# Alignment of 32 sequences: from rows on 32 partitions to four column blocks on 128

## The chip, the cores and the metric

One Trainium2 chip, one core of it. The metric is the device time of one execution in microseconds (us). Engines: PE is TensorE, DVE VectorE, ACT ScalarE, POOL GpSimd, SP SyncE, whose queue issues most DMAs.

## The reference

Two layers with four residual branches over x (32 sequences x 128 tokens x 128) and a context of the same shape:

```python
x = x + tanh(g_xattn[0]) * mlstm(layernorm(x), ctx, ctx)            # 8 heads of 16
x = x + tanh(g_ffn[0])   * quantized_ffn(layernorm(x))              # 128 -> 512 -> 128
x = x + tanh(g_xattn[1]) * align(ctx, layernorm(x))                 # the part that changes
x = x + tanh(g_ffn[1])   * experts(layernorm(x))                    # 8 experts, 128 -> 512 -> 128
```

`align`, for each of the 32 sequences: D[i,j] is the Euclidean distance between context token i and token j of the layer-normed x. R is the dynamic time warping cost, R[i,j] = D[i,j] + min(R[i-1,j], R[i,j-1], R[i-1,j-1]). A backtrack from (127,127) takes the best of diagonal, up and left (in this order when equal), and each row i of the context is added to every column j that the path visits in row i.

## The kernel before, in words

All of x stays in SBUF (`xs`), tokens on partitions. Engines run hand-written programs, each in its own written order, and wait on semaphores. The stages follow one another: mLSTM, quantized ffn, alignment, experts (the second half of the time). The alignment goes like this:

- **Squared distances** (PE L1420 to L1445, ACT L629 to L640, DVE L1052 to L1056). For each group g of four sequences PE turns the layer-normed x, ACT makes -2x and x squared of it (L636, L637), PE sums them with the context, DVE adds the context's norms into `dsq`. ACT takes the root (L640) into `dist`, with tokens i on the partitions. In ACT's order the root of group g-1 stands before the copies of group g+1.
- **Turning** by DRAM: SP writes `dist` to `d_scratch` (L338) and reads it back with the sequences on 32 partitions (`distances`, L334) into `dring`.
- **Row loop** (DVE L1064 to L1088). 128 rows; each is a minimum of the row above with itself shifted by one (L1077) and a `tensor_tensor_scan` with (min, add) over 128 columns (L1081), both on 32 partitions. Each waits for the other's semaphore.
- **Step table** (`back`, L262 to L293). Rows are taken in chunks of 32, 32, 32, 16, 16. SP copies finished rows to 128 partitions, a quarter of the chunk on each 32 (`r9`, L353, L355). DVE then makes MIN, DIAG, LEFT (comparisons), GpSimd the code `ch_k` (L485, L486), DVE a scan with (max, max) (SCAN, L284) and a difference (CUT, L292), which SP brings back to 32 partitions as `kb` (L260). `back_part` puts these parts, of 128 columns each, one behind each minimum and one behind each scan of the next chunk's rows. The last chunk's table is made behind the loop (L1089 to L1100).
- **Tracking** (DVE L1102 to L1110): 128 dependent steps, each a `scalar_tensor_tensor` over 128 columns of `kb` whose sum is the column at which the next row's path ends.
- **Path and sum** (L1111 on): PE turns the ends (L1455), ACT and DVE make 0/1 paths, PE multiplies them with the context (L1463), DVE adds, and the layer norm of the last branch begins.

Beside it the expert weights are prepared (16 tiles of 128x512): ACT issues the loads (`raw_load`, L247), PE turns them (L1452) into banks 4 and 5, ACT copies them to SBUF (L647), GpSimd splits each into a high and a low bf16 part (L475, L476). This begins when the squared distances are done and runs beside the first rows of the loop. Later, `low` (L495) is GpSimd's part of the experts.

Of the kernel before, what the change touches and what calls it, by code (L numbers as in the profile page):

```python
# [5 lines left out]
F32 = mybir.dt.float32  # L6
BF16 = mybir.dt.bfloat16
# [12 lines left out]
E = 8  # L20
# [8 lines left out]
RC = 32  # L29

CHUNKS = [(0, 32), (32, 32), (64, 32), (96, 16), (112, 16)]
NRC = len(CHUNKS)
R9 = 5 * 16


MIN, DIAG, LEFT, SCAN, CUT = range(5)
PLACE_0 = 7
BACK = [sum(5 * rows // 4 for _, rows in CHUNKS[:c]) for c in range(NRC)]
LEFT_DONE = [BACK[c] + 3 * CHUNKS[c][1] // 4 for c in range(NRC - 1)] + [BACK[-1] + 3]
CUT_DONE = [BACK[c] + 5 * CHUNKS[c][1] // 4 for c in range(NRC - 1)] + [BACK[-1] + 6 + CHUNKS[-1][1] // 4]  # L40
# [4 lines left out]
RW = P + 1  # L45


def program(nc, x, ctx_, g_x, g_f, if_w, if_b, on_w, a_w1, a_b1, a_w2, a_b2, gate_w, m_w1, m_b1, m_w2, m_b2, out):
    with ExitStack() as stack:
# [5 lines left out]

        def dram(name, shape, dt):
            return nc.dram_tensor(name, shape, dt)
# [36 lines left out]
        xT2 = Bm[:, 0:1024].rearrange("p (s t) -> p s t", s=2)  # L94
        xTsq = Bm[:, 1024:2048].rearrange("p (s t) -> p s t", s=2)
        dsq = Bm[:, 2048:6144].rearrange("p (b j) -> p b j", b=B)
        dist = Bm[:, 6144:10240].rearrange("p (b j) -> p b j", b=B)

        dring = A[:, 0:8192].rearrange("p (s r j) -> p s r j", s=2, r=RC)
        kb = A[:, 8192:16384].bitcast(BF16).rearrange("p (i j) -> p i j", i=P)  # L100
        rring = Bm[:, 0:2 * (RC + 1) * RW].rearrange("p (s r j) -> p s r j", s=2, r=RC + 1)
        o0 = 2 * (RC + 1) * RW
        r9 = Bm[:, o0:o0 + 9 * RW].rearrange("p (r j) -> p r j", r=9)
        o0 += 9 * RW
        ch_m = Bm[:, o0:o0 + 1024].rearrange("p (r j) -> p r j", r=8)
        ch_g = Bm[:, o0 + 1024:o0 + 2048].rearrange("p (r j) -> p r j", r=8)
        ch_k = Bm[:, o0 + 2048:o0 + 3072].rearrange("p (r j) -> p r j", r=8)
        ch_s = Bm[:, o0 + 3072:o0 + 3072 + 8 * RW].rearrange("p (r j) -> p r j", r=8)
        o0 += 3072 + 8 * RW
        ch_d = Bm[:, o0:o0 + 512].bitcast(BF16).rearrange("p (r j) -> p r j", r=8)  # L110
# [19 lines left out]
        iota2 = sb("iota2", [P, P])  # L130
        ones = sb("ones", [P, P])
# [53 lines left out]
        wraw = slab[:, 0:1024].rearrange("p (s c) -> p s c", s=2)  # L185
        wcp = slab[:, 1024:2048].rearrange("p (s c) -> p s c", s=2)
# [9 lines left out]

        d_dram = dram("d_scratch", (B, P, P), F32).ap()
# [13 lines left out]
            "x3T_turned", "x3T_kept", "dsum_done", "dsq_ready", "dist_ready", "row_done", "rowm_done",  # L211
            "r9_in", "back_done", "k_made", "k_in",
            "track_done", "e_turned", "e_kept", "far_ready", "path_ready", "expanded", "expanded_added",
            "raw_turned", "raw_kept", "w_split",
# [5 lines left out]
        d_out = [sem(f"d_out{c}") for c in range(2)]  # L220
        d_in = [sem(f"d_in{c}") for c in range(2)]
        k_last = [sem(f"k_last{q}") for q in range(4)]
        raw_in = [sem(f"raw_in{c}") for c in range(2)]
# [23 lines left out]
        def raw_load(act, n):  # L247
            if n < E:
                dst, src = four(wraw[:, n % 2, :]), m_w1[n].rearrange("(c p) d -> p c d", c=NC)
            else:  # L250
                dst, src = wraw[:, n % 2, :], m_w2[n - E]
            act.dma_start(dst, src).then_inc(raw_in[n % 2], 16)

        def steps_out(sp, c, parts=range(3, -1, -1)):
            first, rows = CHUNKS[c]
            h = rows // 4
            sp.wait_ge(S["back_done"], CUT_DONE[c])
            for q in parts:
                arrived = S["k_in"] if c < NRC - 1 else k_last[q]
                sp.dma_start(kb[0:B, first + h * q:first + h * q + h], ch_d[32 * q:32 * q + 32, 0:h]).then_inc(arrived, 16)  # L260

        def back(dve, c, stage, q0, q1):  # L262
            h = CHUNKS[c][1] // 4
            q = slice(q0, q1)
            end = c == NRC - 1

            def after(stage):
                dve.wait_ge(S["back_done"], BACK[c] + (stage if end else stage * h + q0) + 1)
            if stage == MIN:
                if q0 == 0:  # L270
                    dve.wait_ge(S["r9_in"], R9 * (c + 1))
                    if c >= 1:
                        dve.wait_ge(S["k_made"], c)
                ins = dve.tensor_tensor(ch_m[:, q], r9[:, q0:q1, 0:P], r9[:, q0:q1, 1:RW], ALU.min)
            elif stage == DIAG:
                ins = dve.tensor_tensor(ch_g[:, q], r9[:, q0:q1, 0:P], r9[:, q0:q1, 1:RW], ALU.is_le)
            elif stage == LEFT:
                after(MIN)
                ins = dve.tensor_tensor(ch_m[:, q], r9[:, q0 + 1:q1 + 1, 0:P], ch_m[:, q], ALU.is_ge)
            elif stage == SCAN:  # L280
                if not end:
                    dve.wait_ge(S["k_made"], c + 1)
                ks = ch_k[:, q].rearrange("p r j -> p (r j)")
                ins = dve.tensor_tensor_scan(ch_s[:, q, 1:RW].rearrange("p r j -> p (r j)"), ks, ks, 0.0, ALU.max, ALU.max)  # L284
            else:
# [4 lines left out]
                if c >= 1:  # L290
                    dve.wait_ge(S["k_in"], 64 * c)
# [1286 lines left out]
```

## Time and profile before

| | us |
|---|---|
| median of 3 runs | 946.1 |
| lowest, highest | 945.65, 1039.48 |
| the profiled execution | 947.22 |
| its span, first to last instruction | 945.5 |
| mean granted TensorE clock in it | 0.804 |

All rows are of the profiled execution; their times count from the start of the span. "32x128 f32" is partitions x elements. A busy time of a group is the union over its instructions; idle time in brackets names the instruction that ended it. PE, PEld (weight load), DVE, ACT and POOL are engines, SPq and ACTq are the queues of SP and ACT that issue DMAs. An fp32 product appears as two records.

### The profile page before, as it was taken

The page shows a single profiled execution, that of the slowest core. Times are in us where ns is not written, and L with a number is a line of the kernel's source. Part 1 is how long each engine was busy: PE and PEld are TensorE (multiplying, and loading weights), DVE is VectorE, ACT ScalarE, POOL GpSimd, SP SyncE. Part 2 cuts the span into 40 slices and gives each one's busy share as a digit, 9 for nine tenths or more (in the row PEclk, how much of TensorE's full clock was granted, in tenths as well). Part 3 has the DMA queues.
Part 4 walks back from the last instruction along what each step waited for, and adds up shares of the span by engine and source line. Part 5 has one row for each costly group of instructions (what it writes and reads, how often), then busy time and mean ns, then how long its engine had stood idle before and what let it go on. Part 6 is the DMA issues. An engine that isn't in the chain of part 4 may idle for free.

```text
span 945.5 us, 16592 instructions
## 1 busy us (share of the span) xinstructions
PE 630.7 (67%) x5620; PEld 432.7 (46%) x5701; DVE 719.7 (76%) x2023; ACT 384.6 (41%) x688; POOL 246.8 (26%) x253
## 2 busy tenths in 40 slices
PE   5968999942525832000000068999999999999998
PEld 4943444421214521000000058677756777777776
DVE  6655678787989569999979885656665878878675
ACT  2344555538852421000000043656554454545453
POOL 1001687851435065201210004877400000000000
PEclk9998999975555955555555565999999999999999
DMA  7000000000000262111110000000000000001000
GB/s 187 23 1 1 1 0 0 0 0 0 1 23 1 79 161 68 41 46 37 25 25 0 0 1 1 1 3 1 2 1 1 13 13 1 11 0 34 0 12 13
DMA packets 26122, 19.61 MB, mean 21 GB/s; under 512 B 2004, under 2 KB 23760, under 8 KB 25936
## 3 DMA queue, kind: packets, MB, share of 16 engines
q1 hardware_dynamic: 20592, 14.65, 6.0%
q10 hardware_dynamic: 5472, 4.26, 1.8%
q8 instruction: 28, 0.46, 0.2%
q14 instruction: 30, 0.25, 0.1%
HBM read 11.21 MB, written 4.19 MB: 16 GB/s over the span
## 4 chain that ended last, share of the span: by engine, by line
PE 57%; DVE 35%; ACT 3%; issue 3%; DMA 2%; SPq 0%; POOL 0%; ACTq 0%; DVEq 0%; POOLq 0%
PE PS L1488 7%; DVE Bm L1081 7%; PE PS L1503 6%; PE PS L1505 6%; PE PS L1504 6%; PE PS L1489 6%; DVE rowm L1077 5%; DVE rowm L1108 5%; PE PS L1487 4%; PE PS L1370 4%; PE PS L1288 3%; PE PS L1344 2%; DVE A L708 2%; DVE hmm L1006 2%; DVE hmm L1007 2%
## 5 line engine op out<-in xcount | busy, mean ns | idle before, releaser
L671 ACT ACTIVATE A<-PS,small_t 128x512 f32<-128x512 f32 x256 | 168.6, 688 | 123.0 <-PE PS L1489 121.5
L1503 PE MATMUL PS<-kT_w,A 128*128 128x128 bf16 x1024 | 174.8, 219 | 0.0
L1504 PE MATMUL PS<-kT_w,A 128*128 128x128 bf16 x1024 | 174.7, 219 | 0.0
L1505 PE MATMUL PS<-kT_w,A 128*128 128x128 bf16 x1024 | 174.7, 219 | 0.0
L1202 DVE TENSOR_TENSOR A<-A 128x512 bf16<-128x512 f32 x192 | 123.6, 690 | 10.5 <-ACT A L671 9.2
L1455 PE MATMUL PS<-identf,ee 32*128 32x32 f32 x1 | 0.3, 312 | 176.6 <-DVE rowm L1108 176.6
L1503 PEld LDWEIGHTS PS<-kT_w,A 128*128 128x128 bf16 x1024 | 100.2, 98 | 11.3 <-issue 4.5
L1504 PEld LDWEIGHTS PS<-kT_w,A 128*128 128x128 bf16 x1024 | 100.2, 98 | 6.6
L1488 PE MATMUL PS<-A,xn_w 128*128 128x512 bf16 (+1 forms) x256 | 97.8, 382 | 3.6 <-issue 0.4
L1505 PEld LDWEIGHTS PS<-kT_w,A 128*128 128x128 bf16 x1024 | 100.2, 98 | 0.0
L1489 PE MATMUL PS<-A,xn_w 128*128 128x512 bf16 (+1 forms) x256 | 97.8, 382 | 0.0
L1210 DVE SCALAR_TENSOR_TENSOR xs<-PS,A,xs 128x128 f32 (+1 forms) x192 | 54.0, 344 | 55.8 <-PE PS L1505 55.8
L653 ACT ACTIVATE Bm<-iota,ec 128x128 f32<-128x128 f32 x32 | 9.5, 386 | 177.4 <-DVE ec L708 177.4
L1455 PEld LDWEIGHTS PS<-identf,ee 32*128 32x128 f32 x1 | 0.2, 178 | 177.0 <-DVE rowm L1108 177.0
L1487 PE MATMUL PS<-A,xn_w 128*128 128x512 bf16 (+1 forms) x193 | 73.8, 382 | 0.0
L495 POOL TENSOR_TENSOR A<-A 128x512 bf16<-128x512 f32 x64 | 64.5, 1041 | 23.3 <-ACT A L671 23.3
L1081 DVE TENSOR_TENSOR_SCAN Bm<-rowm,A 32x128 f32<-32x128 f32 x128 | 67.2, 525 | 2.6
L870 DVE TENSOR_TENSOR Bm<-Bm,PS 128x512 f32<-128x512 f32 x64 | 43.9, 686 | 33.0 <-PE PS L1344 29.6
L1077 DVE TENSOR_TENSOR rowm<-Bm 32x128 f32<-32x128 f32 x128 | 48.6, 380 | 6.9 <-DMA A<-d_scratch 4.4
L572 ACT ACTIVATE Bm<-PS 128x512 f32<-128x512 f32 x64 | 38.2, 597 | 26.2 <-PE PS L1362 26.2
L1108 DVE SCALAR_TENSOR_TENSOR rowm<-iota,ee,A 32x128 f32<-32x128 f32 x128 | 43.5, 340 | 6.3 <-DMA A<-Bm 1.8
L1370 PE MATMUL PS<-slab 32*128 32x256 f32 x256 | 45.9, 435 | 0.0
(273 smaller groups left out, 1332.4 us busy)
## 6 DMA issues: line engine op xcount, KB each, us to landing
slab<-in_L_ffn_w_dram ACTq DMA_DIRECT2D x16, 256.0 KB, 3.0
xs<-in_x_dram SPq DMA_DIRECT2D x4, 512.0 KB, 6.0
cs<-in_ctx_dram SPq DMA_DIRECT2D x4, 512.0 KB, 6.7
d_scratch<-Bm SPq DMA_DIRECT2D x8, 256.0 KB, 2.3
out_dram<-xs SPq DMA_DIRECT2D x8, 256.0 KB, 2.5
Bm<-Bm SPq DMA_DIRECT2D x9, 145.1 KB, 2.4
A<-d_scratch SPq DMA_DIRECT2D x2, 512.0 KB
A<-d_scratch SPq DMA_DIRECT2D x2, 384.0 KB
```

The source lines that it names most:

```text
L671: act.activation(hf[:, e % 2, c, :], bank(c), ACT.Gelu_apprx_tanh, bias=b1).then_inc(S["h_gelu"], 1)
L1077: dve.tensor_tensor(rowm[:], above[:, 1:RW], above[:, 0:P], ALU.min).then_inc(S["rowm_done"], 1)
L1081: dve.tensor_tensor_scan(rring[0:B, c % 2, r + 1, 1:RW], rowm[:], dring[0:B, i // RC % 2, i % RC], BIG, ALU.min, ALU.add)\
L1108: dve.scalar_tensor_tensor(out=rowm[:], in0=iota2[0:B], scalar=ee[:, i + 1:i + 2], in1=kb[0:B, i, :], op0=ALU.is_le, op1=ALU.mult, accum_o ...
L1202: dve.tensor_tensor(hl[:, e % 2, c, :], hf[:, e % 2, c, :], hh[:, e % 2, c, :], ALU.subtract).then_inc(S["h_low_dve"], 1)
L1370: ins = pe.matmul(PS[:, 2 + 2 * half + jj, 0:256], kslot[r, k % 2, :], qslot[r, k % 2], start=True, stop=True)
L1487: pe.matmul(bank(c), w1h[:, e, c, :], x4h[:, xw], start=True, stop=False)
L1488: pe.matmul(bank(c), w1h[:, e, c, :], x4l[:, xw], start=False, stop=False)
L1489: pe.matmul(bank(c), w1l[:, e, c, :], x4h[:, xw], start=False, stop=True).then_inc(S["h_ready"], 1)
L1503: pe.matmul(o, hh[:, e % 2, c, t], w2h[:, e, c, :], start=(c == 0 and k == 0), stop=False, skip_group_check=True)
L1504: pe.matmul(o, hh[:, e % 2, c, t], w2l[:, e, c, :], start=False, stop=False, skip_group_check=True)
L1505: ins = pe.matmul(o, hl[:, e % 2, c, t], w2h[:, e, c, :], start=False, stop=(c == NC - 1), skip_group_check=True)
```

## The change

- **Blocks.** The 128 columns are cut into four blocks of 32, block q on partitions 32q to 32q+31. Block q runs 4q steps behind block 0 (`LAG` = 4), so the loop has 128 + 12 = 140 steps of 128 partitions x 32 columns. The scan's start value is the column 0 of the new row in the table `rt`, in which the last column of the block to the left stands. ACT brings it there: three copies of 32 partitions x 2 rows every two steps (`pass_edges`), for which DVE waits at every second step from step 4 on.
- **Distances.** `dsq` stays as it is and PE turns it: 128 fp32 products with a shifted identity (`idw`), stationary `dsq[:, :, 32q+j]` (a stride of 128 elements), 140 moving columns, four products for the four groups of 32 output partitions, three j to a PSUM bank, 11 banks' worth in four banks. ACT takes the root out of PSUM into `dd`, 11 instructions. The DRAM scratch and its DMAs are gone, and the root no longer stands in the loop over g.
- **Step table.** Made in place, on the same 128 partitions, out of `rt` and the kept minima (`mins`): no MIN part and no `r9`. Chunks of 32, 32, 32, 18, 12, 10, 4 steps. A part is now one instruction for the whole chunk. The code is made by GpSimd for the first four chunks and by DVE for the last three; so is the difference (`steps_of`), before on DVE. A scan with (mult by `resets`, max) gives each block its own maximum; ACT passes the last columns on to the blocks to the right (`pass_tops`, six copies), and DVE joins them (CARRY, TOP). SP brings the differences to `kb`, now in four blocks (q, i, j).
- **Tracking** reads `kb[0:B, :, i]`, four blocks of 32. It waits once, for all of the table.
- **Weights.** SP issues the loads, four buffers. PE turns with products that stay open, ACT copies the high part as bf16, PE subtracts it in PSUM (with a negative identity, `identn`), ACT copies the rest. All but the first two turns come after the row loop in ACT's order. GpSimd has no part in it.
- GpSimd sets up `idw`, `cq`, `rt`, `g_t` and `resets` with memsets during the quantized ffn.

```diff
+LAG = 4
+EACH = 2
+NSTEP = P + 3 * LAG
+CHUNKS = [(0, 32), (32, 64), (64, 96), (96, 114), (114, 126), (126, 136), (136, 140)]
+ON_POOL = 4
+SCAN_AT = [12, 12, 12, 8, 4, 3, 0]
+TOP_AT = [16, 16, 16, 11, 7, 0, 0]
...
+            if stage == DIAG:
+                dve.wait_ge(S["row_done"], b)
+                ins = dve.tensor_tensor(g_t[:, 0:n, 1:RTW], diag, up, ALU.is_le)
             elif stage == LEFT:
+                ins = dve.tensor_tensor(l_t[:, 0:n], left, mins[:, a:b], ALU.is_ge)
...
+                ins = dve.tensor_tensor_scan(flat(top_t[:, 0:n]), flat(resets[:, 0:n]), flat(g_t[:, 0:n]), 0.0, ALU.mult, ALU.max)
+            elif stage == CARRY:
...
+                ins = dve.tensor_reduce(top_t[:, 0:n, 0], cq[:, :, a:b].rearrange("p n s -> p s n"), AX, ALU.max)
+            elif stage == TOP:
+                dve.wait_ge(done, back_at(c, CARRY))
+                ins = dve.tensor_tensor(top, top, carry.to_broadcast([P, n, QC]), ALU.max)
...
+        def back_part(dve, s):
+            for c, (a, b) in enumerate(CHUNKS[:-1]):
+                r = s - b
+                if r == TOP_AT[c] and c < NRC - 2:
+                    back(dve, c, CARRY)
+                    back(dve, c, TOP)
+                    if c >= ON_POOL:
+                        back(dve, c, CUT)
+                for n, stage in enumerate((DIAG, LEFT, CODE, KEEP)):
+                    if r == n and (n < 2 or c >= ON_POOL):
+                        back(dve, c, stage)
+                if r == SCAN_AT[c]:
+                    back(dve, c, SCAN)
...
+            for c in range(ON_POOL):
+                pool.wait_ge(S["back_done"], back_at(c, LEFT))
+                link(code(pool, c))
+                keep_code(pool, c).then_inc(S["k_made"], 1)
+                pool.wait_ge(S["back_done"], back_at(c, TOP))
+                steps_of(pool, c)
...
+            for n in range(TURNS):
+                j0, j1 = JB * n, min(JB * n + JB, QC)
+                act.wait_ge(S["d_turned"], n + 1)
+                own = bank(4 + n % 4, 0, NSTEP * (j1 - j0)).rearrange("p (j s) -> p j s", s=NSTEP)
+                act.activation(dd[:, :, j0:j1].rearrange("p s j -> p j s"), own, ACT.Sqrt).then_inc(S["dist_kept"], 1)
...
+                for q in range(3):
+                    ins = act.activation(rt[32 * q + 32:32 * q + 64, s0 + LAG + 1:s1 + LAG + 1, 0], rt[32 * q:32 * q + 32, s0 + 1:s1 + 1, QC], ACT.Copy)
+                ins.then_inc(S["edge_kept"], 1)
...
+            for s in range(NSTEP):
+                if s:
+                    dve.wait_ge(S["row_done"], s)
+                dve.tensor_tensor(mins[:, s], rt[:, s, 1:RTW], rt[:, s, 0:QC], ALU.min).then_inc(S["min_done"], 1)
+                back_part(dve, s)
+                if s >= LAG and (s - LAG) % EACH == 0:
+                    dve.wait_ge(S["edge_kept"], (s - LAG) // EACH + 1)
+                dve.wait_ge(S["min_done"], s + 1)
+                dve.tensor_tensor_scan(rt[:, s + 1, 1:RTW], mins[:, s], dd[:, s], rt[:, s + 1, 0:1], ALU.min, ALU.add).then_inc(S["row_done"], 1)
...
+            pe.wait_ge(S["turn_ready"], 1)
+            pe.wait_ge(S["dsq_ready"], G4)
+            for n in range(TURNS):
+                if n >= 4:
+                    pe.wait_ge(S["dist_kept"], n - 3)
+                for j in range(JB * n, min(JB * n + JB, QC)):
+                    for q in range(4):
+                        o = NSTEP * (j - JB * n)
+                        ins = pe.matmul(PS[32 * q:32 * q + 32, 4 + n % 4, o:o + NSTEP], dsq[:, :, QC * q + j],
+                                        idw[:, (3 - q) * LAG:(3 - q) * LAG + NSTEP], start=True, stop=True)
+                ins.then_inc(S["d_turned"], 1)
```

## Rows read from the trace of the kernel before

**Rows 1.** Windows: us, busy of PE, PEld, DVE, ACT, POOL, PEclk, DMA share, GB/s

```profile
339.50:369.00 29.50, 11.48 (x44) 8.12 (x44) 28.08 (x41) 7.17 (x12) 21.88 (x25) 0.50 0.45 111
...
339.50:484.10 144.60, 11.48 (x44) 8.12 (x44) 139.30 (x396) 7.17 (x12) 38.67 (x33) 0.50 0.21 50
...
493.60:542.90 49.30, 0.26 (x2) 0.26 (x2) 44.50 (x256) 0.00 (x0) 0.00 (x0) 0.50 0.01 1
```

**Rows 2.** Timeline of DVE, a bare row: start us, length us, line, shapes

```profile
377.35 0.28 DVE L1077 TENSOR_TENSOR rowm<-Bm 32x128 f32<-32x128 f32 x1
377.67 0.41 DVE L1081 TENSOR_TENSOR_SCAN Bm<-rowm,A 32x128 f32<-32x128 f32 x1
378.11 0.28 DVE L1077 TENSOR_TENSOR rowm<-Bm 32x128 f32<-32x128 f32 x1
```

**Rows 3.** Timeline of DVE, a row with two table parts

```profile
389.53 0.27 DVE L1077 TENSOR_TENSOR rowm<-Bm 32x128 f32<-32x128 f32 x1
389.73 0.27 DVE L279 TENSOR_TENSOR Bm<-Bm 128x128 f32<-128x128 f32 x1
389.93 0.41 DVE L1081 TENSOR_TENSOR_SCAN Bm<-rowm,A 32x128 f32<-32x128 f32 x1
...
390.45 0.27 DVE L1077 TENSOR_TENSOR rowm<-Bm 32x128 f32<-32x128 f32 x1
```

**Rows 4.** Timeline, a chunk's code on GpSimd beside the loop

```profile
391.93 2.39 POOL L485 TENSOR_TENSOR Bm<-iota,Bm 128x1024 f32<-128x1024 f32 x1 [23.20 <-DVE Bm L279]
392.21 2.25 DVE L1077 TENSOR_TENSOR rowm<-Bm 32x128 f32<-32x128 f32 x1
...
394.50 2.52 DVE L1081 TENSOR_TENSOR_SCAN Bm<-rowm,A 32x128 f32<-32x128 f32 x1
```

**Rows 5.** Groups of DVE, by form: count, busy us, mean ns, idle before

```profile
L870 DVE TENSOR_TENSOR Bm<-Bm,PS 128x512 f32<-128x512 f32 x64 | 43.9, 686 | 33.0 <-PE PS L1344 29.6 <-ACT Bm L572 3.3
...
L279 DVE TENSOR_TENSOR Bm<-Bm 128x128 f32<-128x128 f32 x28 | 7.0, 266 | 0.0
...
L718 DVE TENSOR_TENSOR lnt<-lnt 128x16 f32<-128x16 f32 x8 | 1.4, 169 | 0.0
...
L708 DVE TENSOR_SCALAR hpos<-hidf,pm 128x8 f32<-128x8 f32 x1 | 0.2, 231 | 0.0
...
L708 DVE TENSOR_SCALAR hneg<-hpos 128x8 f32<-128x8 f32 x1 | 0.2, 171 | 0.0
```

**Rows 6.** Groups of POOL, by form

```profile
L495 POOL TENSOR_TENSOR A<-A 128x512 bf16<-128x512 f32 x64 | 64.5, 1041 | 23.3 <-ACT A L671 23.3
```

**Rows 7.** Groups of ACT, by form

```profile
L515 ACT ACTIVATE lnt<-lnt,cst 128x16 f32<-128x16 f32 x8 | 2.5, 306 | 24.4 <-DVE lnt L720 24.3
...
L522 ACT ACTIVATE tg<-tgr 128x4 f32<-128x4 f32 x1 | 0.2, 205 | 7.4 <-DVE tgr L791 7.4
```

**Rows 8.** Timeline of the squared distances; brackets: idle before, and what ended it

```profile
310.72 1.05 PE L1437 MATMUL PS<-Bm,kT_w 128*128 128x128 f32 x8
...
312.70 0.63 ACT L640 ACTIVATE Bm<-Bm 128x512 f32<-128x512 f32 x1 [5.16 <-DVE Bm L708]
...
314.36 1.12 PE L1434 MATMUL PS<-Bm,ones 128*128 128x512 f32 x2 [2.15 <-ACT Bm L637]
...
328.34 1.13 DVE L708 TENSOR_SCALAR Bm<-PS,aa 128x128 f32<-128x128 f32 x4 [1.06 <-PE PS L1437]
```

**Rows 9.** Timeline of PE in the mLSTM: four products of 32 output rows

```profile
171.89 0.43 PE L1344 MATMUL PS<-Bm 128*32 128x128 f32 x8
172.25 0.33 PE L1351 MATMUL PS<-identf,Bm 128*128 128x128 f32 x1
```

**Rows 10.** The page, granted clock in 40 slices of 23.6 us, in tenths

```profile
PEclk9998999975555955555555565999999999999999
```

**Rows 11.** Timeline behind the last row

```profile
486.25 0.69 DVE L274 TENSOR_TENSOR Bm<-Bm 128x512 f32<-128x512 f32 x1 [2.15 <-DMA Bm<-Bm]
...
491.76 1.42 ACTq L260 DMA_DIRECT2D A<-Bm  x2
```

More of the change, by code:

```diff
@@ L293, in back @@
[L293 to L308 removed]
+                else:
+                    dve.wait_ge(done, back_at(c, KEEP))
@@ new lines, in _, with high, rest @@
+            act.wait_ge(S["rt_ready"], 1)
+            for e in range(GROUPS):
+                pass_edges(e)
+                for c, (a, b) in enumerate(CHUNKS[:-1]):
+                    if e == min((b + SCAN_AT[c] - EACH) // EACH, GROUPS - 1):
+                        pass_tops(c)
+            def high(n):
+                act.wait_ge(S["raw_turned"], n + 1)
+                act.activation(weights(n)[0][:, n % E], four(bank(4 + n % 4)), ACT.Copy).then_inc(S["raw_kept"], 1)
+            def rest(n):
+                act.wait_ge(S["w_left"], n + 1)
+                act.activation(weights(n)[1][:, n % E], four(bank(4 + n % 4)), ACT.Copy).then_inc(S["w_split"], 1)
@@ L650, in _ @@
+            for n in range(2 * E + 1):
+                if n < 2 * E:
+                    high(n)
+                if n >= 1:
+                    rest(n - 1)
             act.wait_ge(S["e_kept"], 1)
@@ L1098, in _ @@
-            for q in range(h):
-                back(dve, c, SCAN, q, q + 1)
-            back(dve, c, CUT, 0, h)
-            for i in reversed(range(P)):
-                first, rows = CHUNKS[-1]
-                if i >= first and (P - 1 - i) % (rows // 4) == 0:
-                    dve.wait_ge(k_last[(i - first) // (rows // 4)], 16)
-                elif i == first - 1:
-                    dve.wait_ge(S["k_in"], 64 * (NRC - 1))
-                dve.scalar_tensor_tensor(out=rowm[:], in0=iota2[0:B], scalar=ee[:, i + 1:i + 2], in1=kb[0:B, i, :],
+            dve.memset(ee[:], 2.0 * (P - 1))
@@ new lines, in _ @@
+            for stage in (DIAG, LEFT):
+                back(dve, NRC - 1, stage)
+            for stage in (CARRY, TOP, CUT):
+                back(dve, NRC - 2, stage)
+            for stage in (CODE, KEEP, SCAN, CARRY, TOP, CUT):
+                back(dve, NRC - 1, stage)
+            for c in (NRC - 2, NRC - 1):
+                dve.wait_ge(k_in[c % 2], K_IN[c])
+            cols = lambda t: t.rearrange("p (q j) -> p q j", q=4)
+            for i in reversed(range(P)):
+                dve.scalar_tensor_tensor(out=cols(rowm[:]), in0=cols(iota2[0:B]), scalar=ee[:, i + 1:i + 2], in1=kb[0:B, :, i],
```

342 lines of the change are left out of this document (144 added, 198 removed).

## The prediction

> **What bounds the kernel now.** I read the stages first, in a table of windows chosen where the work changes [rows 1]. The alignment is one stretch on DVE: 144.6 us for the row loop (DVE busy 139.3 of them, PE 11.5, ACT 7.2), then about 9.5 us that finish the step table, then 49.3 us of tracking with DVE busy 44.5 and every other engine idle. So in this stretch DVE's order is the path, and nothing that PE or ACT do there has a price unless DVE waits for it. The timeline then says what the 144.6 us are made of. A bare row is a minimum of 0.28 us and a scan of 0.41 us, each waiting for the other: 0.76 us from minimum to minimum [rows 2], 97.3 us for 128 rows. Table parts of 128x128 between them cost less than they last: minimum to table part 0.20, to scan 0.20, scan with a second part 0.52, so 0.92 us for a row with two of them, 0.08 each [rows 3]. And twice in a chunk DVE stands still: a minimum that starts during a GpSimd instruction of 2.39 us lasts 2.25 instead of 0.28, the scan behind it 2.52 instead of 0.41 [rows 4]. That is 4.1 us a chunk, three times, and 1.9 for the half chunk: 14 us. The same happens in the first 29.5 us, where GpSimd is busy 21.9 us splitting weights [rows 1]: 20 rows are made there that bare would take 15.2, so another 14 us. Some 28 us of the loop are GpSimd in DVE's way; rows 97, table parts the rest.
>
> **The row loop.** 128 rows of 32x128 become 140 steps of 128x32. A minimum: from 128 to 512 elements a two-input instruction goes from 0.266 to 0.686 us [rows 3, 5], 1.09 ns an element, so 96 elements fewer give 0.278 - 0.105 = 0.173; a 16-wide one measures 0.169 [rows 5], which says that it can't go much lower. I take 0.178. The scan is the term with two readings. At 128 wide it lasts 0.133 more than the minimum [rows 2], which is 1.04 ns an element, the price of one more element-time each; it would be a coincidence if it were a fixed part. So I take 0.411 - 2 x 0.100 = 0.211; with a fixed part it would be 0.311. New is that its start value is read from a column of the table instead of a constant; a scalar from memory shows in two 8-wide instructions, 0.231 with and 0.171 without [rows 5]: plus 0.060. Gaps of 0.032 and 0.035 stay [rows 2]. Step: 0.178 + 0.032 + 0.271 + 0.035 = 0.516 us, x 140 = 72.2 us. Bounds: 0.456 without the 0.060 (64 us) and 0.616 with the fixed part (86 us).
> The Trainium skill ("DVE: opcode table, instruction layouts, handler registers and perf-mode slots", Datapath and trigger behaviour) says that the scan runs at half throughput; this trace has one width and can't show it, but by it the reading per element holds. It also has a rule against this change: "VectorE: DVE Perf Modes", The TRN2 errata, says that many small tiles pay a fixed 151 cycles each; by (32 + 151)/0.96 a minimum would be 191 ns, and the loop 1.8 us longer than here, an estimate; at 128 the same formula gives 291 where the trace has 266 to 278.
>
> **Table parts on DVE.** They now take a whole chunk in one instruction: 32 steps are 1024 elements. In front of a scan there are 0.210 us (minimum to scan, dependent) of which an independent 32-wide one needs about 0.10 [rows 2, 3], so a part of N elements adds about N x 1.04 ns - 0.04: DIAG 1.02, LEFT 1.02, SCAN of 1056 at two element-times 2.16, CARRY with TOP behind it 1.28, together 5.5 us for a chunk of 32. Three such chunks 16.5; the chunk of 18 steps 3.1; that of 12, which makes its code on DVE too, 3.2; that of 10 as far as it lies in the loop 1.8. Sum 24.6 us. Nothing of the old MIN part remains, since the loop keeps its minima.
>
> **GpSimd beside it.** The weight split leaves GpSimd (it becomes PE products and ACT copies after the loop), so the first 14 us of standstill go. But the step code of four chunks stays there and gets a third instruction, the difference (steps_of). Each reads SBUF while DVE runs two-input instructions, which is the case of [rows 4]. Per full chunk 1.97 + 2.11 + 1.97 = 6.05 us, three times 18.2, and 3.1 for the chunk of 18: 21.3 us. Bounds: zero if the new bf16 operands changed the stalling, though the operand count, not the type, is what the stalled rows share; and if the bf16 instructions cost like the one of 512 elements at 1.041 us [rows 6] against 1.2 for half of the 2.39 one, 18 us. I keep 21.3.
>
> **Hand-overs through ACT.** Every second step DVE waits for three ACT copies of 32x2 that carry the edge to the next block. Queued behind this waiting scan is all of DVE's loop. From the row's end to the scan that needs it lie two steps and a minimum, 1.24 us (2 x 0.516 + 0.21). The smallest ACT instruction here is 0.205, a 16-wide one with a root 0.306 [rows 7]; three with two hand-offs of 0.08 are 0.8 to 1.1. Hidden, price 0; without cover it is 68 times the excess. The six copies that carry the table's maxima stand before the next edges in ACT's queue, 1.2 to 1.8 us against four steps (2.1): I give 1 us in all. Loop: 72.2 + 24.6 + 21.3 + 1.0 = 119.1 us against 144.6, **-25.5**.
>
> **Ahead of the loop.** Before, squared distances went through a root on ACT, out to DRAM and back; the last DVE piece of them ends at 329.5 [rows 8] and the loop began at 339.5. Two things move. First, the root stood in ACT's order ahead of the next group's copies: ACT idled 5.16 us for DVE, and PE's product waited 2.15 for ACT [rows 8]. With the roots gone this wait goes, late next is PE itself: squared distances end at 327.3. Shorter waits of later groups I leave out. Second, the turning: 128 fp32 products of 32 output rows, in 32 sets of four with one set of array columns each. The nearest row is the same shape, 128x32 against 128x128: four of them (eight records) take 0.43 us, and the next instruction on the whole array starts 0.36 after the first [rows 9]. For 140 columns 0.39: 32 x 0.39 = 12.5 us. The clock was full (9 tenths) up to that point and PE doesn't pause before it [rows 10]. ACT's 11 roots of 420 elements run beside it at half PE's time; the last adds 0.8 with hand-offs. DVE starts at 327.3 + 12.5 + 0.8 = 340.6, plus 0.3 for the constants added at the start: **+1.4**. Bounds: -2 if sets overlap more; +24 if they run one after another, below.
>
> **The end of the table.** From the last scan (484.1) to the first tracking step it was 9.5 us: 2.15 of waiting for a DMA, table work to 491.7, 1.8 for the DMA home [rows 1, 11]. Now eleven short DVE instructions of 128 to 320 elements, 3.6 us by the prices above; then the last of five DMAs from SP. Four of them are issued 1.9 us before the last table part is ready, at 0.71 us each [rows 11], so the fifth goes 0.9 later and lands 1.9 after that: 6.4 us. **-3.0**.
>
> **Tracking and weights.** The tracking instruction reads four blocks of 32 instead of one of 128. A two-block product elsewhere has the price of a flat one (0.686 for 512) [rows 5], so 0. Bound: +0.1 us a step, 13 us. The 16 weight tiles now pass PE (four fp32 products, 1.05 us at full clock [rows 8], 2.1 at half, and one bf16 product) and two ACT copies of 0.6: 16 x 2.5 = 40 us at half clock, beside 49.3 us of tracking in which both idle [rows 1]. Hidden; had they been exposed they would cost what exceeds 49.
>
> **Sum.** +1.4 - 25.5 - 3.0 = -27.1 us. The profiled execution took 947.22 (span 945.5); it becomes 920.1. The median of the runs is 946.1, 1.1 lower: **919.0 us**. A measurement of this kernel can tell about 2% from no change, that is below 927 or above 965.
>
> **Rivals.**
> (a) The scan's extra is a fixed part, or short instructions cost 0.1 more: +14 for the steps, -4.7 for table scans that get cheaper: 928. For it: no narrow scan in the trace. Against: the coincidence above.
> (b) GpSimd doesn't stop DVE any more: 919 - 21 = 898. For it: operands in bf16. Against: both stalled instructions of [rows 4], and the stalls in the weight split, whose outputs were bf16 already.
> (c) The turning runs set by set without overlap: four full-array fp32 products of 128 columns take 1.05 us at full clock [rows 8], with 140 columns 1.15, so 32 x 1.15 = 36.8 instead of 12.5: 943. For it: the strided stationary operand, which no row has.
> (d) Tracking pays for four blocks: +13, 932.
> (e) The slower side: ACT's edge copies pace the loop. Two steps need 1.03 us; from 0.29 us a copy (3 x 0.29 + 0.16) ACT's own order is longer and each of 68 pairs takes its time. At 0.52 a copy a pair takes 1.72: 68 x 0.69 = 47 us, 966. For it: nothing in the trace moves data between partition groups on ACT. Against: 0.205 and 0.306 [rows 7].
>
> **Chances.** Forecast 0.55 (its own range 908 to 928); (a) 0.13, (b) 0.12, (d) 0.08, (c) 0.06, (e) 0.06. Leaving out most of (b)'s far side, (c) and (e), the range is 900 to 941. Faster: most of the forecast, all of (b), a third of (a), 0.68; within 2%: 0.26; slower: (e), 0.06.
>
> **What would show it.** Right: 128x32 scans near 0.27 and minima near 0.18 with 0.52 between steps; minima or scans of about 2.2 us exactly when GpSimd runs, three times a chunk; PE's turning 12 to 13 us long; no DVE wait for ACT. Wrong: DVE idle before scans with ACT as releaser (e), steps of 0.6 and more (a), 128-partition scans undisturbed beside GpSimd (b), turning sets of 1 us (c), tracking over 0.39 us a step (d), or a PE wait after tracking for the weights.

## The result, and the profile after

The changed kernel takes 917.1 us (three runs, 915.39, 917.12 and 918.83) against 945.65 and 946.1 before: a ratio of 0.9696 [0.9652, 0.9739], 3.0% faster, with 919.0 forecast and 900 to 941 as the range. A second comparison gave 916.25 to 917.31 and 0.9686 [0.9658, 0.9714]. Both kernels also have executions some 93 us longer (1037.88 and 1039.48 before, 1009.62 and 1010.02 after, again 29 us apart), which the forecast left out and which no ratio here uses.

The profiled execution of the changed kernel (1010.02 us, span 1008.2) held the half clock through the mLSTM, well ahead of the alignment, so its alignment begins 92.1 us later than before, while lengths inside it compare directly. The page shows it in the granted clock, where [rows 10] had nines:

```profile
PEclk9995555555555555955555856599999999999999
```

The stages of the alignment as windows (us, busy of PE, PEld, DVE, ACT, POOL, PEclk, DMA share, GB/s): from the last squared distance to the first minimum, the loop of 140 steps, the end of the table, and tracking.

```profile
418.57:428.11 9.54, 7.92 (x257) 7.70 (x257) 0.13 (x2) 8.27 (x11) 0.00 (x0) 1.00 0.02 5
428.11:549.65 121.54, 2.00 (x16) 1.81 (x16) 108.86 (x314) 49.15 (x236) 20.95 (x12) 0.52 0.03 9
549.65:556.00 6.35, 4.23 (x18) 3.94 (x19) 3.12 (x11) 3.91 (x11) 0.00 (x0) 0.50 0.05 12
556.00:606.00 50.00, 16.21 (x110) 14.57 (x111) 44.72 (x257) 14.55 (x27) 0.00 (x0) 0.67 0.22 64
```

Against [rows 1]: the loop is 121.4 us instead of 144.6 (the window closes 0.1 late) and still DVE's; ACT, nearly idle before, is now busy for 49 us of it. Tracking has 44.7 us of DVE against 44.5, with the weights on PE and ACT beside it.

A step without table parts, timeline of DVE (start, length, line, shapes), to be held against [rows 2]:

```profile
454.18 0.19 DVE L1104 TENSOR_TENSOR A<-Bm 128x32 f32<-128x32 f32 x1
454.47 0.28 DVE L1109 TENSOR_TENSOR_SCAN Bm<-A,Bm 128x32 f32<-128x32 f32 x1
454.79 0.19 DVE L1104 TENSOR_TENSOR A<-Bm 128x32 f32<-128x32 f32 x1
455.02 0.28 DVE L1109 TENSOR_TENSOR_SCAN Bm<-A,Bm 128x32 f32<-128x32 f32 x1
455.34 0.19 DVE L1104 TENSOR_TENSOR A<-Bm 128x32 f32<-128x32 f32 x1
```

A step is 0.55 us. Every second one is 0.61: the first scan here starts 0.29 behind its minimum, the other 0.23. The first is the one that waits for the edge as well, and the edge has long been there. No view lists this as a wait, but the trace has an instruction of DVE's queue for it, on the line of the wait for the minimum, 68 times and only ahead of scans that wait for two semaphores (the line's view: shortest, median, longest ns, first and last start):

```profile
L1108 DVEq EVENT_SEMAPHORE  x68: 21/21/21, 430.5 to 547.6; - x68
```

It shows as 0.067 us at 52 of the 68 places. At the other 16 a table part stands between minimum and scan and hides it.

GpSimd beside the loop, timeline of both engines (brackets: idle before, and what ended it), as in [rows 4]:

```profile
449.52 1.96 POOL L266 TENSOR_TENSOR Bm<-iotaq,Bm 128x1024 bf16<-128x1024 bf16 x1 [56.26 <-DVE A L289]
...
449.66 1.86 DVE L1104 TENSOR_TENSOR A<-Bm 128x32 f32<-128x32 f32 x1
451.55 1.96 POOL L270 TENSOR_TENSOR Bm<-Bm,A 128x1024 bf16<-128x1024 bf16 x1
451.63 1.97 DVE L1109 TENSOR_TENSOR_SCAN Bm<-A,Bm 128x32 f32<-128x32 f32 x1
...
464.88 1.89 POOL L276 TENSOR_TENSOR Bm<-A 128x1024 bf16<-128x1024 f32 x1 [11.37 <-DVE A L311]
465.03 1.79 DVE L1104 TENSOR_TENSOR A<-Bm 128x32 f32<-128x32 f32 x1
```

Three GpSimd instructions a chunk, and each holds a DVE instruction of 0.19 or 0.28 until it ends. What it costs stands in the groups of DVE in the loop (count, busy us, mean ns, idle before):

```profile
L1109 DVE TENSOR_TENSOR_SCAN Bm<-A,Bm 128x32 f32<-128x32 f32 x140 | 45.4, 324 | 7.6
L1104 DVE TENSOR_TENSOR A<-Bm 128x32 f32<-128x32 f32 x140 | 38.4, 274 | 14.2 <-ACT A L647 9.4
L303 DVE TENSOR_TENSOR_SCAN A<-Bm 128x1056 f32<-128x1056 bf16 x3 | 7.1, 2350 | 0.0
L311 DVE TENSOR_TENSOR A<-A 128x1024 f32<-128x1024 f32 x3 | 3.7, 1226 | 0.1
L287 DVE TENSOR_TENSOR Bm<-Bm 128x1024 bf16<-128x1024 f32 x3 | 3.7, 1218 | 0.0
```

Undisturbed, 140 scans of 0.284 and 140 minima of 0.192 are 66.6 us; they last 83.8, so 17.2 us are standstill.

The way into the loop: DVE's last squared distances, ACT's roots, DVE's first minimum (timeline), and PE's turning (the line's view: shortest, median, longest ns, first and last start).

```profile
417.45 1.12 DVE L746 TENSOR_SCALAR Bm<-PS,aa 128x128 f32<-128x128 f32 x4 [0.63 <-PE PS L1450]
...
419.74 8.27 ACT L647 ACTIVATE A<-PS 128x420 f32<-128x420 f32 x11 [4.71 <-PE PS L1468]
...
428.11 0.19 DVE L1104 TENSOR_TENSOR A<-Bm 128x32 f32<-128x32 f32 x1 [9.41 <-ACT A L647]
```

```profile
L1468 PE MATMUL PS<-A,Bm x256: 282/283/348, 418.7 to 426.3; 128*32 128x140 f32 x128
```

The 32 sets take 7.9 us, 0.246 each, so three sets, one root's worth, take 0.72. ACT's 11 roots run without a gap and start every 0.77, a little slower than that, and they end 1.4 us behind PE's last product. One root is longer than the distance between two of them, since they overlap (the line's view; the short one is the last, of 280 elements):

```profile
L647 ACT ACTIVATE A<-PS x11: 663/975/1012, 419.7 to 427.3; 128x420 f32<-128x420 f32 x10, 128x280 f32<-128x280 f32 x1
```

ACT's groups around the loop, and behind it the end of the table (timeline; SPq is SP's queue):

```profile
L653 ACT ACTIVATE Bm<-Bm 32x2 f32<-32x2 f32 x204 | 41.6, 204 | 62.2 <-DVE Bm L1109 60.4
```

```profile
545.54 9.50 SPq L362 DMA_DIRECT2D A<-Bm  x7
...
549.25 0.26 DVE L1109 TENSOR_TENSOR_SCAN Bm<-A,Bm 128x32 f32<-128x32 f32 x1
...
550.73 0.19 DVE L308 TENSOR_REDUCE A<-A 128x10 f32<-128x30 bf16 x1 [0.69 <-ACT A L664]
...
556.25 0.34 DVE L1121 SCALAR_TENSOR_TENSOR rowm<-iota,ee,A 32x128 f32<-32x128 f32 x1 [2.55 <-DMA A<-Bm]
```

An edge copy is 0.204 us. From the last scan (549.5) to the first tracking step it is 6.7 us instead of 9.5, the last 2.55 of them for the DMA that brings the table home.

The three stages together: ahead of the loop, from PE's second turn of four sequences (305.33 before, 397.44 here) to the first minimum, 34.2 us became 30.7 (-3.5); the loop -23.2; the end of the table -2.8. Sum -29.5; the runs say -29.0. Nothing is left for the rest: tracking lasts 49.03 us in both traces, and from its end to the end of the program it is 402.9 in both.

### The profile page after: what moved, and what is told of

Its sections match the earlier page's. It is cut to its first block, busy times and chain, and to the rows that moved or that the text cites. A ratio compares the mean times of both kernels' runs of the same rounds, so it can differ in the third digit from the quotient of the medians.

```text
span 1008.2 us, 17409 instructions
## 1 busy us (share of the span) xinstructions
PE 738.0 (73%) x5953; PEld 475.6 (47%) x6037; DVE 677.2 (67%) x1940; ACT 447.1 (44%) x947; POOL 225.2 (22%) x234
## 4 chain that ended last, share of the span: by engine, by line
PE 59%; DVE 25%; issue 4%; ACT 3%; SPq 0%; DMA 0%; DVEq 0%; POOL 0%; ACTq 0%; POOLq 0%
PE PS L1383 7%; PE PS L1526 7%; PE PS L1541 6%; PE PS L1542 6%; PE PS L1543 6%; PE PS L1527 5%; DVE Bm L1109 5%; DVE rowm L1121 5%; PE PS L1525 4%; DVE A L1104 4%; PE PS L1357 4%; PE PS L1373 3%; PE PS L1375 3%; PE PS L1364 2%; PE PS L1372 2%
## 5 line engine op out<-in xcount | busy, mean ns | idle before, releaser
L1478 PE MATMUL PS<-identf,slab 128*128 128x128 f32 x128 | 20.2, 311 | 125.3 <-ACT xn_w L676 121.7
L1383 PE MATMUL PS<-slab 32*128 32x256 f32 x256 | 78.3, 710 | 0.2 <-DVE slab L746 0.2
L653 ACT ACTIVATE Bm<-Bm 32x2 f32<-32x2 f32 x204 | 41.6, 204 | 62.2 <-DVE Bm L1109 60.4
L1484 PEld LDWEIGHTS PS<-xn_w,identn 128*128 128x128 bf16 x8 | 1.0, 125 | 121.4 <-ACT xn_w L676 121.4
L1383 PEld LDWEIGHTS PS<-slab 32*128 32x128 f32 x256 | 32.3, 308 | 53.4 <-DVE Bm L910 29.3
L567 ACT ACTIVATE Bm<-PS 128x128 f32<-128x128 f32 x64 | 17.8, 278 | 74.2 <-PE PS L1357 74.2
L1109 DVE TENSOR_TENSOR_SCAN Bm<-A,Bm 128x32 f32<-128x32 f32 x140 | 45.4, 324 | 7.6
```

The lines of the kernel that those rows point to most:

```text
L1109: dve.tensor_tensor_scan(rt[:, s + 1, 1:RTW], mins[:, s], dd[:, s], rt[:, s + 1, 0:1], ALU.min, ALU.add).then_inc(S["row_done"], 1)
L1383: ins = pe.matmul(PS[:, 2 + 2 * half + jj, 0:256], kslot[r, k % 2, :], qslot[r, k % 2], start=True, stop=True)
```

## The experiments

Each ran beside the kernel before on the same chip.

**The change again**, for a narrower interval and beside the first variants.

> The changed kernel itself, for a second profile. Theory: about 917 us; PE's turning 7.9 us and 9.5 us from the last squared distance to the first minimum, the loop 121.5 us, 6.6 us from the last scan to tracking, as in its first profile, since nothing in these stretches depends on PE's clock before them. Rival: the first profile's mLSTM ran at the half clock (the record says 5 tenths there), and if that state lasts into the alignment, then these stretches get shorter here, by up to half of PE's 7.9 us.

917.31, 916.72 and 916.25 us, as said above. The other runs are held against 917. The second trace has the lengths of the first: 7.9 us of turning, 9.5 from the last squared distance to the first minimum, 121.4 for the loop, 6.7 for the end of the table. Its mLSTM ran at the half clock too, so by itself it can't answer the rival; the trace of the version with all parts together, further down, has the full clock in most of its mLSTM and the same 7.9 us of turning.

**GpSimd out of the loop.** The step code of all chunks on DVE.

```diff
-ON_POOL = 4
+ON_POOL = 0
```

> ON_POOL = 0: DVE makes the code and the differences of all chunks, GpSimd nothing in the loop. Theory (a GpSimd instruction that reads SBUF stops DVE's two-input instructions for its whole length): the standstills of 1.77 + 1.77 + 1.60 us a full chunk go (1.86 and 1.97 and 1.79 instead of 0.19, 0.28, 0.19), 15.4 us for three and about 2.6 for the chunk of 18, 18 in all; DVE takes on three instructions a chunk, the two bf16 ones at 0.33 us for 320 elements, so about 0.6 us of issue for 1024, and the f32 difference 1.1: 2.3 a full chunk, 8.2 in all. Net -9 to -11 us, about 907. Rival (the standstill only replaces waiting that DVE would do anyway, for ACT's edges or its own results): the work added counts in full and the time rises by about 8, to 925.

907.03 us, and 905.85 on the repeat below. Groups of DVE:

```profile
L1109 DVE TENSOR_TENSOR_SCAN Bm<-A,Bm 128x32 f32<-128x32 f32 x140 | 39.4, 281 | 7.0
L1104 DVE TENSOR_TENSOR A<-Bm 128x32 f32<-128x32 f32 x140 | 26.9, 192 | 14.1 <-ACT A L647 9.3
...
L276 DVE TENSOR_TENSOR Bm<-A 128x1024 bf16<-128x1024 f32 x3 | 3.7, 1225 | 0.1
L266 DVE TENSOR_TENSOR Bm<-iotaq,Bm 128x1024 bf16<-128x1024 bf16 x3 | 2.1, 701 | 0.0
```

The pairs lose 17.5 us (83.8 to 66.3). What comes back on DVE: twelve instructions, 2.63 us for each full chunk and 1.68 for the fourth, 9.6 in all; each starts under the instruction before it and fills a gap, which is worth some 0.2 (at the end of the loop a part of 0.48 adds 0.28 between minimum and scan). So 7.2 come back by this reckoning, 10.3 are gained, and the runs show 10 to 11; the loop itself is 111.7 us in both traces of this version against 121.4, 9.7 less. The standstill is shown, and so is that it costs more than the work it was meant to save.

**The weights alone.** The kernel before, with nothing changed but the weight split, taken to PE and ACT as in the change (four buffers, as there) and left beside the loop. The code shows a part of the edit; PE's products are not in it.

```diff
+            pool.tensor_scalar(identn[:], identb[:], -1.0, 0.0, ALU.mult, ALU.add)
...
-            for n in range(2 * E):
-                split_weights(n)
...
-                act.activation(wcp[:, n % 2, :], bank(4 + n % 2), ACT.Copy).then_inc(S["raw_kept"], 1)
+                act.activation(weights(n)[0][:, n % E], four(bank(4 + n % 4)), ACT.Copy).then_inc(S["raw_kept"], 1)
...
+            def rest(n):
+                act.wait_ge(S["w_left"], n + 1)
+                act.activation(weights(n)[1][:, n % E], four(bank(4 + n % 4)), ACT.Copy).then_inc(S["w_split"], 1)
```

> The kernel before with one part of the change alone: the expert weights are split by PE and ACT (four buffers, loads still issued by ACT, done beside the row loop) instead of by GpSimd. Theory: the 20 rows that took 29.5 us take 15.2, so -14 us: 932, which is half of the whole gain. Rival (the new alignment alone brings the gain; the weights beside it only used time in which DVE waited for its own results): within 3 us of 946.

932.55, 934.84 and 935.84 us, ratio 0.9873 [0.9828, 0.9918], 12 us less. The window of its row loop, to be held against the 144.60 of [rows 1]:

```profile
339.10:469.40 130.30, 15.15 (x82) 12.95 (x82) 125.04 (x396) 10.16 (x19) 16.78 (x8) 0.54 0.20 48
```

The loop is 14.3 us shorter with its rows unchanged. Ahead of it this version is 2.4 us slower than before (41.9 us from PE's first turn to the first minimum, against 39.4), which leaves the 12 of the runs; why it is slower there stays open. Of the change's 29 us, then, 12 to 14 are not owed to the four blocks at all, but to GpSimd's leaving the first 29.5 us of the loop. The blocks, the turning and the table in place bring the other 15 to 17.

**Edges every four steps.** Half as many hand-overs, but the copies then have no step between them and the scan that needs them.

```diff
-EACH = 2
+EACH = 4
```

> EACH = 4: the edge is handed on every fourth step, with the same lag of four, so the hand-over has a minimum as its only cover. Theory: three copies at 0.21 us spacing and two hand-offs are 0.8 us from the end of the scan to the next permitted one; 0.23 of it lie beside the minimum, so about 0.55 us are exposed at 34 places, +19, less 34 second waits of 0.06, -2: +14 to +18 us, about 933. Rival (the copies, not their latency, are what ACT's path is short of; half as many instructions are quicker): within 3 us of the changed kernel or faster.

926.02 and 926.06 us, ratio 0.9784: 9 more than the change, half of what was expected. Waits of DVE, and one of them in the timeline:

```profile
DVE Bm L1109 <- ACT Bm L653: 12.4, 23, 1.2
```

```profile
434.24 0.65 ACT L653 ACTIVATE Bm<-Bm 32x4 f32<-32x4 f32 x3 [1.99 <-DVE Bm L1109]
...
434.92 0.28 DVE L1109 TENSOR_TENSOR_SCAN Bm<-A,Bm 128x32 f32<-128x32 f32 x1 [0.49 <-ACT Bm L653]
```

An exposed hand-over holds the scan 0.45 us longer than the minimum would, and it shows at 23 places: 10.4 us, less 29 second waits of 0.067 that showed in the change and are gone, 1.9, gives 8.5. The loop in the trace is 130.0 us, 8.6 longer than the change's. With a hand-over every two steps the same three copies are hidden: after the row's end DVE has 1.4 us of its own before it needs them, and they take 0.64. This is the mechanism of rival (e), brought about by an edit; at 0.204 a copy the change was far from its 0.29.

**The edge wait ahead of the minimum.** I took the 0.06 us of every second step for a second wait between minimum and scan, on the path, and put it where DVE waits for the row anyway.

```diff
+                if s >= LAG and (s - LAG) % EACH == 0:
+                    dve.wait_ge(S["edge_kept"], (s - LAG) // EACH + 1)
                 dve.tensor_tensor(mins[:, s], rt[:, s, 1:RTW], rt[:, s, 0:QC], ALU.min).then_inc(S["min_done"], 1)
                 back_part(dve, s)
-                if s >= LAG and (s - LAG) % EACH == 0:
-                    dve.wait_ge(S["edge_kept"], (s - LAG) // EACH + 1)
```

> The wait for ACT's edges stands ahead of the minimum instead of ahead of the scan; nothing else differs. In the changed kernel the scan behind such a wait starts 0.10 us after the minimum's end instead of 0.04, though the edges came long before (68 places, 4.1 us). Theory (the second wait in front of one instruction is what costs, since the first is over before it can be taken; ahead of the minimum it is taken while the scan of 0.28 us runs): -3 to -4 us, about 913. Rival (the edges really come late, and the profile's ends hide it): the wait moves ahead by 0.25 us and stalls more, +5 us or more.

921.18 us, 4 more than the change: the sign was wrong. Timeline:

```profile
455.24 0.64 ACT L653 ACTIVATE Bm<-Bm 32x2 f32<-32x2 f32 x3 [0.53 <-DVE Bm L1109]
455.31 0.19 DVE L1106 TENSOR_TENSOR A<-Bm 128x32 f32<-128x32 f32 x1
455.53 0.28 DVE L1109 TENSOR_TENSOR_SCAN Bm<-A,Bm 128x32 f32<-128x32 f32 x1
...
456.47 0.19 DVE L1106 TENSOR_TENSOR A<-Bm 128x32 f32<-128x32 f32 x1
```

The scan is back at 0.23 behind the minimum, but the minimum now starts 0.07 behind the release of the scan before it (455.24, where ACT is released) instead of together with it. Two steps last 1.16 as before. So the extra wait costs its 0.07 in front of the minimum as well, and there no table part hides it: it shows at all 68 places instead of 52, 1.1 us more. Standing earlier it is also met earlier: DVE waits 1.3 us in all for edges that are not there yet. Together 2.4 us, and the loop in the trace is 123.9 us, 2.5 longer than the change's. The other 1.5 us of the 4, one time against three, stay open.

**Forms of the scan.** A probe: every fourth step with a constant start value, and every fourth split into two scans of 16 columns, so its blocks don't continue each other.

```diff
+                if s % 4 == 1:
+                    dve.tensor_tensor_scan(rt[:, s + 1, 1:RTW], mins[:, s], dd[:, s], BIG, ALU.min, ALU.add).then_inc(S["row_done"], 1)
+                elif s % 4 == 3:
+                    link(dve.tensor_tensor_scan(rt[:, s + 1, 1:17], mins[:, s, 0:16], dd[:, s, 0:16], rt[:, s + 1, 0:1], ALU.min, ALU.add))
+                    dve.tensor_tensor_scan(rt[:, s + 1, 17:RTW], mins[:, s, 16:QC], dd[:, s, 16:QC], BIG, ALU.min, ALU.add).then_inc(S["row_done"], 1)
...
```

> A measurement of the scan's price; at every fourth step its start value is a constant (the blocks then don't continue each other), and at every fourth the row is made in two scans of 16 columns, the first with its start value from the table, the second with a constant; the distances' path is another one then. Theory (two element-times an element, 0.06 for a start value from memory): 128x32 with a constant 0.22 us against 0.284, 128x16 with a constant 0.19, 128x16 from the table 0.25. Rival (one element-time and a fixed extra of 0.13): 128x16 is only 0.017 shorter than 128x32, 0.267 from the table. Second rival: the start value costs nothing, 128x32 stays at 0.28.

Groups of DVE (L1115 is the plain form, with GpSimd's standstill in its mean; undisturbed it is 0.284):

```profile
L1115 DVE TENSOR_TENSOR_SCAN Bm<-A,Bm 128x32 f32<-128x32 f32 x70 | 25.4, 363 | 5.5
...
L1112 DVE TENSOR_TENSOR_SCAN Bm<-A,Bm 128x16 f32<-128x16 f32 x35 | 8.8, 251 | 1.1
L1110 DVE TENSOR_TENSOR_SCAN Bm<-A 128x32 f32<-128x32 f32 x35 | 7.8, 223 | 1.0
L1113 DVE TENSOR_TENSOR_SCAN Bm<-A 128x16 f32<-128x16 f32 x35 | 7.7, 219 | 1.2
```

The last mean holds one standstill beside GpSimd as well, as the line's view shows (shortest, median, longest ns):

```profile
L1113 DVE TENSOR_TENSOR_SCAN Bm<-A x35: 192/193/1110, 429.2 to 553.2; 128x16 f32<-128x16 f32 x35
```

Undisturbed this form is 0.193. A start value from the table costs 0.284 - 0.223 = 0.061 us at 32 columns, as forecast. Between 16 and 32 columns lie 0.033 with it (0.251 to 0.284) and 0.030 with a constant (0.193 to 0.223), 1.9 to 2.1 ns a column, so two element-times of 1.04 in both forms. All three expected lengths are met, and both rivals are out.

**Roots written flat.** In the change ACT writes its roots with a stride; here `dd` is laid out as PSUM has it, the scan reads it with the stride, and the minima get a place of their own. The line that writes is shown.

```diff
-                act.activation(dd[:, :, j0:j1].rearrange("p s j -> p j s"), own, ACT.Sqrt).then_inc(S["dist_kept"], 1)
+                act.activation(dd[:, j0:j1, :], own, ACT.Sqrt).then_inc(S["dist_kept"], 1)
```

> ACT writes the roots of the turned distances in the order in which PE made them (column by column, 140 steps in a row) and the scans read them with a stride of 140 elements; the minima get a place of their own. In the changed kernel each of ACT's 11 roots of 420 elements takes 0.75 us with single elements 128 bytes apart, and PE's turning of 7.9 us ends just before ACT. Theory (the strided write sets ACT's pace, and ACT the start of the loop): 0.5 us a root, so PE's 7.9 us become the limit; the loop starts 0.4 to 1.0 us earlier, scans unchanged at 0.284: about 916. Rival (a strided read slows the scan, which is two element-times now): +0.03 us or more a step, +4 us.

914.76 and 919.0 us, within the spread of the change. The trace has the small gain that the runs can't tell: DVE's wait for the last root,

```profile
DVE Bm L1104 <- ACT A L647: 8.5, 1, 8.5
```

is 0.9 us shorter (it was 9.4), the loop is 121.5 us long, and the scans last the same as before, stride or not.

**All together.** Code on DVE, the edge wait first, flat roots, and the table of maxima in bf16 so that its two instructions (TOP, L311, and CUT, L276) might last as little as the bf16 ones of the code, 0.70 us for 1024 elements instead of 1.22.

> Code and differences on DVE, the edge wait first, flat roots, and the table of maxima (top_t) kept as bf16, so that DVE's TOP and CUT read and write 16-bit numbers only. Theory: -10 (measured for the code on DVE), -4, -0.6, and 0.5 us less for each TOP and CUT of 1024 elements, the bf16 code instruction of that size taking 0.70 us where the f32 ones take 1.23: 9 such instructions' worth, -4 to -5. About 898, 19 below the changed kernel. Rival (the carried value of TOP is read with a stride of zero and keeps that instruction at one element a cycle): 2 us less gain, 900.

907.76 and 909.18 us, ratio 0.9599 [0.9573, 0.9624]: 10 us more than expected, and nothing gained over the code on DVE alone (907.03). The early wait is a part of the reason: the loop is 113.0 us here and 111.7 with the code on DVE alone. ACT's roots, timeline:

```profile
331.29 0.53 ACT L647 ACTIVATE A<-PS 128x420 f32<-128x420 f32 x1 [0.17 <-PE PS L1468]
```

Flat, a root is 0.53 long instead of 0.98, and each waits for PE. So PE is late next: the roots now start every 0.72 us, PE's pace, instead of every 0.77, and the last one ends sooner, which together is the 0.9 of the run before.

**The same without the early wait**, and the code on DVE a second time.

```diff
-                if s >= LAG and (s - LAG) % EACH == 0:
-                    dve.wait_ge(S["edge_kept"], (s - LAG) // EACH + 1)
                 dve.tensor_tensor(mins[:, s], rt[:, s, 1:RTW], rt[:, s, 0:QC], ALU.min).then_inc(S["min_done"], 1)
                 back_part(dve, s)
+                if s >= LAG and (s - LAG) % EACH == 0:
+                    dve.wait_ge(S["edge_kept"], (s - LAG) // EACH + 1)
```

> The changed kernel with all step code on DVE, roots written flat, the table of maxima in bf16, and the wait for the edge where the change has it, behind the minimum. Theory: the parts measured so far add: step code on DVE -9.5 (907 against 917), flat roots -1 (0.9 less waiting ahead of the loop), 4.4 cuts that are 0.5 shorter -2, and none of the +1.4 to +4 that the early wait cost: 904 to 905, and steps that stand 0.06 further apart only every second time. Rival: the early wait costs nothing beside this order of table parts (e.g. ACT's six copies are late either way), then it stays at 907 to 909 as all together, and waits of DVE for ACT of 1 us and more stay.

> The changed kernel with the step code of all chunks on DVE, a second time, beside the run above on the same chip: 907 and a ratio near 0.959 to the kernel before, if the single undisturbed time stands; the run above then is 2 to 3 us faster. If it is 910 or more, the gain of moving the code off GpSimd was overstated and the parts do add in the version with all of them.

904.82, 905.5 and 905.67 us, ratio 0.9562 [0.9542, 0.9583], the fastest version here; the code on DVE alone 905.85, after 907.03. Against all together, the early wait cost 3 us, as its own run had said; in the traces the loop went from 113.0 to 109.8 us, which is the same 3.2. Groups of DVE of the first:

```profile
L311 DVE TENSOR_TENSOR A<-A 128x1024 bf16<-128x1024 bf16 x3 | 3.7, 1224 | 0.1
L276 DVE TENSOR_TENSOR Bm<-A 128x1024 bf16<-128x1024 bf16 x3 | 2.2, 724 | 0.1
```

In bf16 CUT fell from 1.225 to 0.724, TOP stayed: one of its inputs is a single value per step, repeated 32 times. Shorter roots and cuts are 3 us by the traces (the loop 1.9, the start 0.8, the end of the table 0.1 less than with the code on DVE alone); the runs show 1.1 over the mean of the two times without them, less than this spread can settle.

## What held of the prediction, and which of its steps failed

**The bound** was read rightly: DVE's order stayed the path through loop and tracking, and the work that was put on PE and ACT beside it cost nothing itself. The sum of -27.1 stands against -29.5 in the trace. That the total came so near is in part luck: its terms were off by up to 5 us each, some one way and some the other.

**The steps that failed.** Two are mechanisms. Ahead of the loop the prediction had +1.4 us and the runs showed -3.5, the other direction: it took the turning as 32 x 0.39 = 12.5 us with ACT's roots beside it at half PE's time, where the turning took 7.9 and ACT was the slower one. And it put the wait for an edge that is already there at nothing, where it costs 0.067 us at 52 places. The other failures are sizes: the step, 0.516 us forecast and 0.55 measured, and the standstill beside GpSimd, 21.3 and 17.2. One by one:

- **The step, 0.516 us, was 0.55.** The minimum was mis-sized: 0.178 forecast, 0.192 measured. I went down a line from 512 and 128 elements and preferred a 16-wide 0.169 as its floor. The rule of the Trainium skill that I cited ("VectorE: DVE Perf Modes", The TRN2 errata), 151 cycles fixed, gives 191 ns, and the trace agrees to within 1 ns. I had set it aside because it gives 291 at 128 columns where [rows 3, 5] have 266; that it misses one row didn't make my line through two others right at a third width. Behind the changed loop the 128-element ones are 0.28 to 0.29 us, so at that width there are rows for either. The scan was 0.284 instead of 0.271, off by the same 0.013; both parts of its price hold up: two element-times a column and 0.061 for the start value. Rival (a), a fixed part of 0.1 more, is out. 140 steps: 77.0 us instead of 72.2.
- **The hand-overs, 1.0 us, cost 3.5**, and not in the way that I looked for. ACT's copies are hidden as forecast (0.204, no wait recorded in the loop). But the scan had to ask for two semaphores, and the second question is 0.067 us at 52 places. It is in no list of waits, but the alternation of 0.23 and 0.29 shows it. Where the change added a wait I asked whether it would be long, and not what a wait costs that is already met. The Trainium skill ("Perfetto Trace Analysis", Identifying Dependency Chains) says that an instruction that waits on several engines may get an extra semaphore instruction ahead of it; it gives no price. The traces here agree, with the one of L1108 above, and put it at 0.067.
- **The standstill beside GpSimd, 21.3 us, was 17.2.** The mechanism is shown (without GpSimd all 140 minima are 0.19), bf16 or not, so rival (b) is out. The term was mis-sized: the GpSimd instructions of 1024 bf16 elements last 1.96 us and not 2.39, and a stall is their length less the time by which DVE starts into them, 1.6 to 1.7 each.
- **The table parts, 24.6 us,** are what is left: 121.4 - 77.0 - 3.5 - 17.2 = 23.7. The long scan, 2.35 for 1056 elements, and 1.22 for 1024 are near their forecast.
- **Turning, 12.5 us, was 7.9.** I took the 0.36 to 0.43 of one isolated set of four [rows 9] as the rate of 32 sets in a row; that is a latency. Back to back they come every 0.246, less than one full-array product of 140 columns would take by [rows 8] (1.05 / 4 x 140 / 128 = 0.287). The Trainium skill ("TensorE: Matmul & The Clock Gate", Measured speedup vs the span model) says that a pack spans one product and some 4 ns for each further tile; by it and [rows 8] the estimate would have been 32 x 0.30 = 9.6, closer than mine, and the trace has still less. Since PE was faster than I thought, ACT became the pace, if by little: its strided roots, which I had put at half PE's time, start every 0.77 against PE's 0.72, and take 8.3 in a row. The working also says that the clock was full up to that point; [rows 10] have half of it in the four slices before the squared distances. Through the turning it was full (1.00 in the window above), so no term hangs on it. Rival (c) is out. With squared distances 3.0 us shorter instead of 2.2 (I had left out the short waits of later groups), the start gained 3.5 where I had it lose 1.4.
- **The end of the table,** 6.7 against 6.4, and **tracking,** unchanged at 49 us with four blocks to read, went as forecast; rival (d) is out. The weights did fit beside it: tracking lasts 49.03 us with and without them, and what follows it 402.9.
- **The weights' share,** 14 us of standstill in the first 29.5 us, was read rightly: moved alone, they shortened the loop by 14.3.

The step 4.8 and the waits 2.5 too low, the end of the table 0.3 too low, standstill 4.1, parts 0.9 and the start 4.9 too high: the forecast lies 2 us from the runs in part because these cancel. By the traces alone no single term was off by more than 5 us.

What the profile of before held and I didn't use: the forecast kept 21 us of standstill as given. Taking the code off GpSimd is one line and was worth 10 to 11 of them, over a third of what the whole change brought.

## What to carry to other kernels

An instruction of GpSimd that reads SBUF beside a DVE chain of short two-input instructions must be priced as time in DVE's order, its length less the time by which DVE starts into it: compare that with what the same work takes on DVE, here 0.7 to 1.2 us against 1.6 to 1.7. In a chain of steps of half a microsecond a second wait, even a met one, and a start value from memory each have a price (0.067 and 0.061 us here), so count semaphores per step as you count instructions. A mean over a group can hide one disturbed instruction among many, so read the median before you explain a number. And take the rate of packed products from a run of them, and a narrow instruction's price from a narrow one; single sets and extrapolated lines were the two terms that missed.

## What the runs showed of the hardware

- A wait that is already fulfilled costs DVE 0.067 us when the instruction already has another, ahead of the minimum as well as ahead of the scan. The trace has an instruction of DVE's queue for it (0.021 us long), and a table part of 0.29 us or more between the two instructions hides it.
- Three edge copies between partition groups on ACT take 0.64 us, 0.204 for 32x2 and nearly the same for 32x4 (0.65 for three): between two and four columns size doesn't matter, count does.
- ACT's root of 420 elements from PSUM is 0.98 us long (median of 11) written with a stride of 32 elements, with starts 0.77 apart, and 0.54 written flat. DVE's scan shows no such difference when it reads the same table with a stride of 140: 0.281 on average either way (code on DVE alone, and all together).
- DVE instructions of 1024 bf16 elements run at about 0.70 to 0.72 us instead of 1.22, though their rows start at odd places (33 elements a row, from the first or the second). The Trainium skill ("VectorE: DVE Perf Modes", Mode 2×_1P) asks for steps of one and for starts on 4 bytes; the trace agrees on the step, since TOP with its repeated input stays at 1.224, and not on the starts.
